# First projections that also stack the first head pair in SBUF and take 28 of the 32 maxima of the attention's first block of keys

## The reference, cut to what matters

```
x = layernorm(x)                       # (1, 4096, 256)
q = split_heads(x @ Wq.T + bq)
k = split_heads(x @ Wk.T + bk)
v = split_heads(x @ Wv.T + bv)
scores = einsum('hbnd,hbmd->hbnm', k, q) * SCALE
attn = softmax(scores, axis=-1)        # over the 4096 queries m, for every key n
out = einsum('hbnm,hbmd->hbnd', attn, v)
```

## Time and profile before

| what | value |
|---|---|
| median of 3 runs | 4578.8 us |
| the profiled execution's own time | 4585.69 us |
| its span | 4583.8 us |
| PE busy | 4338.3 us (95%) |
| DVE busy | 3556.6 us (78%) |
| ACT busy | 3062.9 us (67%) |
| POOL busy | 911.3 us (20%) |
| mean granted clock of TensorE | 0.968 of full speed |

### The profile page before, as it was taken

How to read it: one execution, slowest core, us unless ns; L and a number is a source line. 1 busy time by engine, 2 the same in 40 slices (tenths; PEclk the granted TensorE clock), 3 DMA queues, 4 the chain that set the end, 5 groups by cost and what they waited for, 6 DMA issues and landing times. The chain is left out here.

```text
span 4583.8 us, 107739 instructions
## 1 busy us (share of the span) xinstructions
PE 4338.3 (95%) x36307; PEld 2678.2 (58%) x36307; DVE 3556.6 (78%) x4059; ACT 3062.9 (67%) x5552; POOL 911.3 (20%) x1768
## 2 busy tenths in 40 slices
PE   6599999999999999999999978999988799999999
PEld 5244444444444444444444437888867678888887
DVE  5699999999999999999999976565544655555554
ACT  2188888888888888887888865444455454444444
POOL 5211111211211212111111110000001222222222
PEclk8699999999999999999999989999988899999999
DMA  5410200200202001002112122000010522222222
GB/s 186 97 19 13 30 13 13 31 13 13 31 13 31 13 13 31 13 13 63 43 32 50 33 69 70 28 28 27 14 37 14 182 81 83 86 84 84 88 88 89
DMA packets 237634, 225.10 MB, mean 49 GB/s; under 512 B 129024, under 2 KB 197552, under 8 KB 236096
## 3 DMA queue, kind: packets, MB, share of 16 engines
q1 hardware_dynamic: 195840, 142.47, 12.8%
q0 software_dynamic: 41344, 76.61, 5.5%
HBM read 174.67 MB, written 60.36 MB: 51 GB/s over the span
## 5 line engine op out<-in xcount | busy, mean ns | idle before, releaser
L824 DVE TENSOR_REDUCE PM<-A 128x2 f32<-128x1024 f32 x2092 | 2456.2, 1221 | 112.9 <-PE A L713 79.8
L801 ACT ACTIVATE PR<-SB 128x512 f32<-128x512 f32 x4100 | 2121.2, 602 | 361.2 <-PE SB L726 349.5
L746 PE MATMUL PV<-PR,VH 128*32 128x256 f32 x16384 | 1292.6, 386 | 1.5 <-issue 1.5
L713 PE MATMUL A<-QST,KA 48*128 48x512 f32 x4184 | 1192.1, 475 | 59.8 <-DMA QF<-QFD 34.2
L746 PEld LDWEIGHTS PV<-PR,VH 128*32 128x32 f32 x16384 | 432.1, 110 | 553.4 <-issue 367.1
L713 PEld LDWEIGHTS A<-QST,KA 48*128 48x128 f32 x4184 | 426.1, 186 | 518.8 <-issue 412.7
L726 PE MATMUL SB<-KST,QST 50*128 50x512 f32 x3075 | 686.0, 410 | 0.1
L726 PEld LDWEIGHTS SB<-KST,QST 50*128 50x128 f32 x3075 | 386.1, 186 | 205.9 <-ACT PR L801 202.9
L734 PE MATMUL SB<-KF,QF 99*32 99x512 bf16 x4100 | 414.5, 384 | 6.3 <-issue 4.1
L2066 DVE TENSOR_TENSOR m_h_lo<-m_h,m_h_hi 128x512 fp32r<-128x512 f32 x320 | 221.4, 692 | 251.0 <-ACT m_h_hi L1974 251.0
L1974 ACT CAST m_h_hi<-m_h 128x512 fp32r<-128x512 f32 x320 | 187.9, 587 | 259.0 <-DVE m_h L2063 257.0
(11 more groups left out here) (278 smaller groups left out, 5677.6 us busy)
## 6 DMA issues: line engine op xcount, KB each, us to landing
m_shares<-CW POOLq DMA_DIRECT2D x512, 128.0 KB, 2.9
QST<-QS SPq DMA_DIRECT2D x54, 256.0 KB, 8.8
KST<-KS SPq DMA_DIRECT2D x402, 32.0 KB, 1.8
QS<-parts SPq DMA_DIRECT2D x16, 512.0 KB, 5.1
KS<-parts SPq DMA_DIRECT2D x16, 512.0 KB, 5.0
m_x<-X SPq DMA_DIRECT2D x16, 512.0 KB, 4.0
moe_w_lo<-W SPq DMA_DIRECT2D x16, 512.0 KB, 10.1
KF<-KFD SPq DMA_DIRECT2D x402, 16.0 KB, 1.8
```

The lines of the kernel that those rows point to most:

```text
L713: return nc.tensor.matmul(A[:, u % 2 * 2 + e, :], keys, QST[rows, slot, j * TB:(j + 1) * TB], start=True, stop=True)
L746: mm = nc.tensor.matmul(PV[at:at + 2 * HD, 0:HB], VH[:, slot, e, c, :], PR[:, (2 * c + e) % P_SLOTS, b * HB:(b + 1) * HB], start=(c == 0), ...
L801: nc.scalar.activation(PR[:, v % P_SLOTS, :], SB[:, s_bank(v), :], ACT.Exp, scale=SCALE).then_inc(s_free, 1)
L824: nc.vector.tensor_reduce(PM[:, par, :, i, j:j + 1], A[:, u % 2 * 2:u % 2 * 2 + 2, :], AX.X, ALU.max).then_inc(a_free, 1)
```

## The change

The first projections also build what the attention's start needs, and the attention's start no longer loads it. In the order of the diff:

- `unrolled` takes the place of `overlapped` in this phase: the eight blocks stand one after the other, without a loop.
- `qk_ps` has 2 banks rather than 4 (projections c and c + 2 share one); the two banks freed are `first_ps`.
- SP, after the store of the fine keys of block i, issues `stacks`: 6 DMAs from `parts` into `QST` and 6 from the fine queries into `QF`; for blocks 0, 1 and 2 also 6 into `KST` and 6 into `KF`. All go from SBUF to SBUF. The `KST` ones count on the same semaphore as the `QST` ones.
- POOL deals the keys of blocks 0 and 1 into `KA` at the start of blocks 1 and 2, ahead of its fine parts.
- In block i, PE makes the four units (key quarter n = 0 to 3) of the first block of keys against the queries of block i - 1 (`first_scores`): the first after projection c = 1, the others after c = 3, after the first half of the values, and at the end. The first waits until all stacks of block i - 1 have landed, each of the others until the maximum before it is done. DVE takes the maxima (`first_maximum`) after `low` of c = 1, of c = 3, and after each half of the values' bias. That makes 7 x 4 = 28 units.
- The attention starts without its 48 loads and with the 4 units against the last block of queries.

```
+def unrolled(body):
+    for i in range(NB):
+        body(i // 2, i, i % 2, 2 if i + 2 < NB else NB - 1 - i)
...
+        first_ps = ps("first_ps", [P, 2, TB])
...
+        def early_keys(i):
+            return i < 3
...
+        def qk_stores(i):
+            return of_slot(i, lambda j: 4 + 2 * len(Q_PARTS) + (2 * len(K_PARTS) if early_keys(j) else 0))
...
+                    stacks(i, slot, 0, QST[:, 0, ds(i, TB)], Q_PARTS, QF[:, 0, ds(i, OB)], 1, FINE_Q)
+                    if early_keys(i):
+                        stacks(i, slot, 2, KST[:, i, :], K_PARTS, KF[:, i, :], 3, FINE_K)
+
+                def stacks(i, slot, c, stack, order, fine_stack, fine_c, fine_order):
+
+                    for e in range(2):
+                        for r, j in enumerate(order):
+                            at = e * HALF + r * HD
+                            sp.dma_start(stack[at:at + HD, :].bitcast(F32), parts[slot][0:HD, c + e, j, :].bitcast(F32)
+                                         ).then_inc(qk_stored[slot], 16)
+                    for r, j in enumerate(fine_order):
+                        sp.dma_start(fine_stack[r * HD:(r + 1) * HD, :], fine[slot][fine_c][0:HD, j, :]
+                                     ).then_inc(fine_stored[slot], 16)
...
                 def blocks(half, i, slot, following):
                     pe.wait_ge(ln.lo_ready, count(i + 1))
-                    for c in range(4):
-                        queries_keys(i, slot, c)
+                    queries_keys(i, slot, 0)
+                    queries_keys(i, slot, 1)
+                    first_scores(i - 1, 0)
+                    queries_keys(i, slot, 2)
+                    queries_keys(i, slot, 3)
+                    first_scores(i - 1, 1)
                     values(i, slot, 0)
+                    first_scores(i - 1, 2)
                     if following:
                         ln.tensor_turn(pe, i + 1)
                     values(i, slot, 1)
+                    first_scores(i - 1, 3)
+
+                def first_scores(j, n):
+
+                    if j < 0:
+                        return
+                    if n == 0:
+                        pe.wait_ge(dealt, count(2))
+                        pe.wait_ge(qk_stored[j % 2], count(qk_stores(j)))
+                    pe.wait_ge(first_free, count(j * TT + n))
+                    for e in range(2):
+                        rows = slice(e * HALF, e * HALF + STACK)
+                        mm = nc.tensor.matmul(first_ps[:, e, :], KA[rows, 0, n * P:(n + 1) * P],
+                                              QST[rows, 0, ds(j, TB)], start=True, stop=True)
+                    mm.then_inc(first_done, 1)
...
                 def blocks(half, i, slot, following):
+                    if i:
+                        deal(i - 1)
                     fine_parts(half, i, slot, 0, 1)
                     fine_parts(half, i, slot, 1, 3)
 
+                def deal(b):
+
+                    if b >= 2:
+                        return
+                    pool.wait_ge(qk_stored[b], count(qk_stores(b)))
+                    for e in range(2):
+                        rows = slice(e * HALF, e * HALF + STACK)
+                        nc.gpsimd.tensor_copy(KA[rows, b, :].rearrange("p (i q) -> p i q", i=TT),
+                                              KST[rows, b, :].rearrange("p (q i) -> p i q", i=TT)).then_inc(dealt, 1)
...
                     low(i, slot, 1)
+                    first_maximum(i - 1, 0)
                     low(i, slot, 2)
                     if following:
                         ln.vector_normalize(dve, i + 1, x_tok[1 - slot])
                     low(i, slot, 3)
+                    first_maximum(i - 1, 1)
                     values(i, 0)
+                    first_maximum(i - 1, 2)
                     if following:
                         ln.vector_lo(dve, i + 1, 1 - slot)
                     values(i, 1)
+                    first_maximum(i - 1, 3)
...
-                load_k(0, 0)
-                load_q(0, 0)
-                load_k(0, 1)
-                load_k(0, 2)
+                for nb in range(3):
+                    sp.sem_inc(k_loaded[nb], K_LOAD)
+                sp.sem_inc(q_loaded[0], Q_LOAD)
                 load_shift(0, 0)
...
                 pe.wait_ge(q_loaded[0], count(Q_LOAD))
-                pe.wait_ge(ka_ready, count(2))
-                for u in range(MC):
-                    units_a(0, u, 0, 0)
                 pe.wait_ge(ka_ready, count(4))
+                for n in range(TT):
+                    pe.wait_ge(a_free, count(EARLY_A + n + 1))
+                    for e in range(2):
+                        rows = slice(e * HALF, e * HALF + STACK)
+                        mm = nc.tensor.matmul(A[:, n % 2 * 2 + e, :], KA[rows, 0, n * P:(n + 1) * P],
+                                              QST[rows, 0, T - TB:T], start=True, stop=True)
+                    mm.then_inc(a_done, 1)
...
                 pool.wait_ge(ones_set, count(1))
-                for b in range(2):
-                    pool.wait_ge(k_loaded[b], count(K_LOAD))
-                    deal(b, b)
+                pool.sem_inc(ka_ready, 4)
                 values_of(0, 0)
                 shift_parts(0, 0)
```

More of the change, by code:

```diff
@@ L409, in high @@
                     act.wait_ge(qk_done, count(i * 4 + (c + 1)))
-                    act.wait_ge(qk_stored[slot], count(half * 64))
+                    if i >= 2:
+                        act.wait_ge(qk_stored[slot], count(qk_stores(i - 2)))
                     if c == 1:
@@ L414, in high @@
                         act.wait_ge(summed, count(i * 2 + 2))
-                    nc.scalar.activation(parts[slot][:, c, 0, :], qk_ps[:, c, :], ACT.Identity,
+                    nc.scalar.activation(parts[slot][:, c, 0, :], qk_ps[:, c % QK_BANKS, :], ACT.Identity,
                                          bias=qk_bias[:, c:c + 1]).then_inc(high_ready, 1)
@@ L430, in _ @@
                 act.wait_ge(bias_loaded, count(48))
[L431 removed]
+                unrolled(blocks)
             @block.gpsimd
@@ L447, in fine_parts @@
                     pool.wait_ge(low_ready, count(i * 4 + (c + 1) + QK_BANKS))
-                    pool.wait_ge(fine_stored[slot], count(half * 32))
+                    if i >= 2:
+                        pool.wait_ge(fine_stored[slot], count(fine_stores(i - 2)))
                     pool.wait_ge(fine_ready, count(k * FINE))
@@ L478, in low @@
                     nc.vector.scalar_tensor_tensor(
-                        out=parts[slot][:, c, 1, :], in0=qk_ps[:, c, :], scalar=qk_bias[:, c:c + 1],
+                        out=parts[slot][:, c, 1, :], in0=qk_ps[:, c % QK_BANKS, :], scalar=qk_bias[:, c:c + 1],
                         in1=parts[slot][:, c, 0, :].bitcast(F32), op0=ALU.add,
@@ L503, in blocks, with first_maximum @@
                     values(i, 1)
+                    first_maximum(i - 1, 3)
+                def first_maximum(j, n):
+                    if j < 0:
+                        return
+                    dve.wait_ge(first_done, count(j * TT + (n + 1)))
+                    nc.vector.tensor_reduce(PM[:, 0, :, n, j:j + 1], first_ps[:, :, :], AX.X,
+                                            ALU.max).then_inc(first_free, 1)
                 dve.sem_inc(low_ready, QK_BANKS)
@@ L510, in _ @@
                 dve.wait_ge(bias_loaded, count(48))
-                overlapped(dve, blocks)
+                unrolled(blocks)
 MC = T // P
@@ L832, in block_max @@
                                             AX.X, ALU.max, negate=True).then_inc(neg_ready, 1)
-                dve.sem_inc(a_free, 2)
+                dve.sem_inc(a_done, EARLY_A)
+                dve.sem_inc(a_free, EARLY_A + 2)
+                for n in range(TT):
+                    dve.wait_ge(a_done, count(EARLY_A + n + 1))
+                    nc.vector.tensor_reduce(PM[:, 0, :, n, NB - 1:NB], A[:, n % 2 * 2:n % 2 * 2 + 2, :], AX.X,
+                                            ALU.max).then_inc(a_free, 1)
+                shift_of(0, 0)
                 with dve.Fori(0, STEPS // 2) as two:
-                    for par in range(2):
-                        block_max(two * 2 + par, par)
-                block_max(STEPS, 0)
+                    for n in range(2):
+                        block_max(two * 2 + (n + 1), 1 - n)
                 for u in range(LEAD + 2):
```

43 lines of the change are left out of this document (26 added, 17 removed).

## The result

The changed kernel takes 4629.8 us (median of 6 runs, 4625.6 to 4639.4) against 4581.2 for the kernel before (6 runs, 4578.3 to 4584.0): 1.0105 times as long, 95% interval 1.0095 to 1.0115. It is 48.6 us slower where 18 were forecast, and outside the range. The span of its profiled execution is 4627.8 us, 44.0 more than before.

The account below looks back on a forecast made before the run. The prediction took PE and DVE to bound the steady attention, loads then DVE its start, a chain through all engines the projections. Start 64.3 us later less 52.7 gained (+11.6), plus 4.5 and 2 of clock: +18, 4597 us; range 4581 to 4615.

Parts of the forecast that it names:

- the change leaves that part alone, so only its start can move: Steady attention, PE busy 99.94 of 100 us: claimed untouched by the change, so only the attention's start could shift.
- SP's issues: Projections, SP issuing stacks: 0.46 us per DMA, six in 2.77 us, 12 more (5.5 us) where keys are stacked.
- The dearer rival: Projections: PE at 1.2 GHz throughout and SP at 0.5 per DMA, +34, 4613 us; chance 0.17, with a lost wait.
- the ring: Projections, PE's wait for stacks through ACT, DVE, POOL, SP and landing: 18.2 us a block, 23.7 with keys stacked.
- 64.3 + 4.5 + 2: Attention's start: 64.3 us later with PE at 2.4 GHz, plus 4.5 and 2 for PE's slower clock.
- The gain at the start: Attention's start: dropping the loads and 28 of 32 maxima cuts 60.2 us to 7.5, gaining 52.7.
- Behind the reduction nothing changes: Attention's start, from reduction to first exponential: ten units of the second block and the shift's DMAs stay 13.1 us.
- PE at 1.2 GHz behind the long waits: Projections, first scores where keys are stacked: matmuls 0.42 apart instead of 0.24, 1.5 us a block, 4.5 for three.
- The two banks of `qk_ps` at nothing: Projections: two banks fewer cost nothing, as c = 2 waits for the first `low`, past when the stack lands.
- The rival in which the stacks are never last: Projections: stacks land early and DVE sets 16.1 us a block; -25, 4554 us; chance 0.08.
- The rule on the receipt: Stacks' landing: a skill's rule read as shorter SBUF to SBUF landings, about 7 us back; not used in the forecast.
- The cheaper stacks: Projections, SP: a DMA without a DRAM address costs 0.37 to issue; +8, 4587 us; chance 0.2.

Follow-up runs that it names:

- e4: The kernel before with `unrolled` alone, the projections' eight blocks written out, no stacks or maxima there: 4598.3 us, 1.0039 of before.
- e1: The kernel before with 80 small matmuls more on PE ahead of the attention's loop: 4603.5 us, 1.0049 of before.
- e2: The changed kernel with 48 small matmuls more on PE at the start of the attention: 4609.9 us, 1.0063 of before.
- e3: The changed kernel with the stacks of parts (`QST`, `KST`) issued ahead of the stores `QFD` and `KFD`: 4594.2 us, 1.0030 of before.
- e9: The changed kernel with the `KST` DMAs ahead of the `QF` ones in blocks 0 to 2: 4622.4 us, 1.0087 of before.
- e8: The changed kernel without `first_scores` and `first_maximum`, all 32 maxima made in the attention: 4630.2 us, 1.0111 of before.
- e5: The kernel before with the load of the next pair's queries spread, two DMAs in each of six steps: 4570.1 us, 0.9977 of before.
- e7: e3 with the load of the next pair's queries spread, two DMAs in each of six steps: 4567.8 us, 0.9977 of before.
- e10: e7 with 48 small matmuls more on PE at the start of the attention: 4563.0 us, 0.9960 of before.
- e11: e10 with the keys of blocks 1 and 2 loaded from DRAM in blocks 3 and 4, second deal in block 6: 4556.3 us, 0.9951 of before.
- e6: The changed kernel with the load of the next pair's queries spread, two DMAs in each of six steps: 4607.4 us, 1.0060 of before.

## Why the prediction was wrong

**The step that failed** is "the change leaves that part alone, so only its start can move". It left the steady attention's work alone, not its place: `unrolled` moved PE's loop from 355 to 579 matmuls into the program, and the loop took 21.4 us more in the trace. e4 makes that move alone (+17 in the median), e1 shifts the loop by idle matmuls alone (+22), e2 shifts that of after (-20). It is more than twice the error in the projections, and no rival had it. The trace of before had the sign of it, the 2.95 us stop for "issue" at the branch back, and I passed over it.

**A term mis-sized: SP's issues.** I took 0.46 each from the stacks' relatives that read DRAM; they took 0.63. For 90 on the chain that is 15 us. The trace of before had the price, in the shift's SBUF to SBUF DMAs at 208.85, which I used only for their landing. The dearer rival had such a term (0.5, +4) and was still too low. With 0.63 the ring comes to 19.7 us for queries alone (18.2 + 6 x 0.17 + 0.5 of clock; measured 19.3 on the mean) and 28.5 with keys (23.9 + 18 x 0.17 + 1.5; measured 27.9). So its other terms together were 0.4 to 0.6 too large, some 3 us over seven blocks. The projections also begin 1.8 us earlier (55.15 for 56.93), most of which isn't the change's doing: e1 and e4 have 55.9 and 56.1. In all the start came 8.9 later than 64.3 + 4.5 + 2. That it missed by no more is in part luck: some 5 us of small errors went against the 15 of the issues.

**What held.** The gain at the start (52.7; 52.6). "Behind the reduction nothing changes": 13.1 us from the reduction to the exponential, 13.2 now. The ring through PE's wait on the stacks, with long waits while keys are stacked and some 4 us later. The landings at 2.0 and 1.8. PE at 1.2 GHz behind the long waits. The two banks of `qk_ps` at nothing: between 55 and 229 PE never waits for `low`. e3 and e9 shorten this ring where it was said to run. But it isn't all of the stacks' price, as I had put it: e8 shows that without PE's wait the blocks are still 14.5 us at the least against 12.5 before, and 27.6 at the most, since other waits for the stacks stand close behind PE's. The rival in which the stacks are never last had 16.1 us for a block; in blocks 4 to 7 of e3, where PE doesn't wait for them, a block takes 14.5 to 16.5.

**The rule on the receipt.** The rows of after decide it: SBUF to SBUF lands in 1.8 to 2.0 us, no sooner than `KST<-KS` from DRAM. The shorter landing that I read out of "DMA: Bandwidth & Descriptors", "Anatomy of one DMA", of the Trainium skill isn't there, and keeping the rows was right. The rule speaks of the memory that is written, and that is SBUF in both rows, so it gave no ground for a shorter landing; that section is also on DMAs that GpSimd issues, and these are SP's. The cheaper stacks had their sign wrong: these DMAs are dearer to issue.

**What stays open.** That the load of the queries makes a packet of PE's instructions late is shown by e5 to e7, e10 and e11; by what way it does so in the DMA engines isn't, and neither is why a late packet stops PE at one place and mostly not at another. At the branch back PE stops twice where 67 matmuls modulo 128 lie ahead of the loop (after, e3, e4, e6 to e9) and once at 51, 99 and 115 (a further stop there, some 20 us later, goes with a late packet); the reason wasn't found. Of the loop's 21.4 us, place is 17 to 22 by the medians; whether a few us are something else can't be told from single traces. The 4.4 us that after gains behind the loop are within what the 13 traces show there (1872.7 to 1877.9; e4, without stacks, has 1872.7), so they need not come from the stacks.

## What to carry to other kernels

A loop written out, or matmuls added, ahead of a long hardware loop move that loop's code in PE's instruction stream; before blaming the work, look in the loop for stops whose releaser is "issue", and try padding, or spreading the DMA bursts beside them. Price a DMA's issue by rows with the same source and target memory, and count what stands behind it in the issuing queue: 24 more DMAs ahead of a load made DVE wait 5.5 us for it, 12 more 2.4 to 2.6 (e8). A copy that reads a double buffer also holds its writer back (ACT's waits in e8). Data that is needed late is cheaper loaded late (e11), and stacks that need only the first product of a chain shouldn't stand behind its last (e3, 35 us).

## What the runs showed of the hardware

- SP issues a DMA of 16 partitions every 0.46 us from DRAM to SBUF and every 0.63 us from SBUF to SBUF (medians of after), the latter for 8, 16 and 32 KB alike. Those of 8 to 32 KB landed in 1.7 to 2.0 us either way.
- PE's instruction packets (16.4 KB, one in 10.1 us of the attention's loop) come over DMA too. Where twelve loads of queries kept the DMA engines at a share of 0.98, the next packet came 13.8 to 19.9 us after the last, with the loads spread 10.6 to 12.1. All 25 times of 17 us and over go with a stop of PE, of 1.0 to 2.5 us.
- The branch back of the attention's loop stops PE for 2.7 to 4.6 us once, or a second time for 1.9 to 3.0, and its step takes 4 to 13 us more. Whether once or twice depends on the number of instructions ahead of the loop: 48 or 80 small matmuls moved the kernel by 20 and 22 us.
- A stop costs more than its length: behind PE's 1.99 us in after the granted clock was 0.50 for 2 us and 0.72 for 2 more; behind the two stops of e6 (6.3 us together) it was 0.50 up to 886.
